# Mixing the work lists of 128 lanes before sorting them again, and issuing the index spread ahead of a group's fetches

## Chip, cores and metric

One core of one Trainium2 chip. The metric is device time in microseconds (us) of one execution; the time before is a median of three runs.

## What is computed

A two-layer network over 64 samples of 256 tokens with 256 features, so 16,384 tokens. Layer 0 is a graph convolution and an LSTM, layer 1 a graph convolution and a feed-forward block. The change touches one piece of that last block, the "tropical" product, which takes a maximum where a matrix product takes a sum:

```python
def blk_fn(xx):                                   # xx: tokens x 256, after a layer norm
    t = jnp.max(xx[:, None, :] + Wt[None, :, :], axis=-1) + bt     # tokens x 1024
    z = t[:, :, None]
    cvx = jnp.max(z * sl_cvx[None] + of_cvx[None], axis=-1)
    ccv = jnp.min(z * sl_ccv[None] + of_ccv[None], axis=-1)
    return s * cvx + (1.0 - s) * ccv
trop = jax.lax.map(blk_fn, xb).reshape(T, FFN)
classical = jax.nn.gelu(xf @ Wc + bc, approximate=False)
g = jax.nn.sigmoid(xf @ Wg + bg)
out = (g * trop + (1.0 - g) * classical) @ Wd + bd
```

The tokens that reach it are normalised rows of a network that starts from normally distributed inputs. The only parts that treat the position of a token in its sample differently are the LSTM and its running sums, which enter with weights near 0.001.

## The kernel before

The tropical product is not computed over all 256 features. For a token, only features whose value plus the largest weight of that feature is high can hold the maximum. `tropical_first` handles the four best features of each half (128 features, `k` = 0 or 1) of all tokens and counts in `done_count[lane, tile, k]` how many of the 128 features of each half are thereby proved irrelevant; a token-half with less than 128 is open, and 128 minus the count is how many features it still needs. Token `128 * tile + lane` sits on lane (partition) `lane`; there are `TILES` = 128 tiles, so each lane has a list of 128 token-halves for each half.

`tropical_plan` (DVE, with two small turns on PE) builds a key from the need and the tile number, counts per lane how many keys need more than 8, 6, 4, 3, 2 and 0 features, takes the maximum over the 128 lanes of each count, and sorts each lane's list in descending order (16 rounds of `max`, which finds eight, and `match_replace`, which strikes them out). Nothing else runs beside it.

`tropical_slots` then runs once for each half. A slot takes the next entry of each lane's sorted list, so one slot works on 128 token-halves. `CLASSES = (16, 8, 6, 4, 3, 2)`: a slot of class g fetches g features for every lane. The number of slots up to the end of each class is the longest lane's count, rounded up to an even number (slots run in pairs) and at least two more than the class before. Each class is a loop of its own on PE, ACT, DVE and POOL.

- DVE: `select` finds the eight (or sixteen) best features of a slot (`ts_top`, `ts_place`) and writes their numbers to `ts_cand` (L2169). `use` (L2180) merges one fetched column of 1024 into the result.
- PE: `spread` (L2103) turns the numbers of a group of up to four features into `ts_index`; it waits for `selected`, that is for the `select` of the slot that it belongs to. `fetch` (L2112) is four matmuls of 512 columns, one-hot times weights, into one of three `ts_fetched` buffers (`RING = 3`); it waits until DVE has used what was in the buffer.
- ACT: `turn_hot` (L2084, L2087) makes `ts_onehot` of the index.
- POOL: for each slot a gather of `t`, a gather of the inputs `y` for three slots on, and a scatter of the result.

The order on DVE is written by hand. Before each slot's uses stands the select of the next:

```python
for j in range(2):
    dve.wait_ge(fetched_used, first + j * g + RING)
    select(i + j + 1, 1 - j, (i + 2 * j) * 8 + 16, 2 if g > CAND else 1)
    for c in range(g):
        use(first, j, g, c, (i + 2) * 8)
```

`tropical_general` treats token-halves that need more than 16 features (here a single placeholder round), and the feed-forward stage follows.

Of the kernel before, what the change touches and what calls it, by code (L numbers as in the profile page):

```python
# [6 lines left out]
F32 = mybir.dt.float32  # L7
BF16 = mybir.dt.bfloat16
F32R = mybir.dt.float32r
ALU = mybir.AluOpType  # L10
ACT = mybir.ActivationFunctionType
AX = mybir.AxisListType
ds = bass.ds

P = 128
B, N, D = 64, 256, 256
KD = D // P
NT = N // P
TOK = B * N
# [1256 lines left out]
CAND = 8  # L1276
TILES = TOK // P
# [8 lines left out]
STEEPEST = 40.0  # L1286
EXP_SPAN = 74.0
ROUND = 12582912.0
FT8 = FFN // P
CH = 512  # L1290
GRP = 4
# [556 lines left out]
def tropical_plan(nc, v):  # L1848


    with ExitStack() as ctx:
        def sb(name, shape, dt=F32):
            return ctx.enter_context(nc.sbuf_tensor("tp_" + name, shape, dt))

        def sem(name):
            return ctx.enter_context(nc.semaphore("tp_" + name))
# [4 lines left out]
        key, left_key, sorted_key = (sb(n, [P, KD, TILES]) for n in ("key", "leftkey", "sortedkey"))  # L1861
        above = sb("above", [P, C, TILES])
        whole, is_open = sb("whole", [P, KD, TILES]), sb("isopen", [P, KD, TILES])
        order, row, from_row, no_token, no_token2 = (
            sb(n, [P, KD, SLOTS]) for n in ("order", "row", "fromrow", "notoken", "notoken2"))
        count, most = sb("count", [P, C]), sb("most", [C, 1])
# [2 lines left out]
        dense = sb("dense", [1, 2])  # L1869
        ps_count = ctx.enter_context(nc.psum_tensor("tp_pscount", [C, P], F32))  # L1870
        ps_most = ctx.enter_context(nc.psum_tensor("tp_psmost", [1, C], F32))
        done_count, rows, ident = (v[n] for n in ("done_count", "rows", "ident"))
        counted, count_turned, most_ready, most_turned = (
            sem(n) for n in ("counted", "count_turned", "most_ready", "most_turned"))
        steps = Steps(sem("steps"), 1)
        block = ctx.enter_context(nc.Block())

        @block.tensor
        def _(pe):
            pe.wait_ge(counted, 1)  # L1880
            pe.transpose(ps_count[:, :], count[:, :], ident[:, :]).then_inc(count_turned, 1)
            pe.wait_ge(most_ready, 1)
            pe.transpose(ps_most[:, :], most[:, :], ident[0:C, 0:C]).then_inc(most_turned, 1)

        @block.vector
        def _(dve):
            def then(instruction):

                dve.wait_ge(steps.sem, steps.done(instruction))

            steps.begin(0)
            then(dve.tensor_scalar(key[:, :, :], done_count[:, :].rearrange("p (s k) -> p k s", k=KD),
                                   -2.0 * P, 2.0 * P * P, ALU.mult, ALU.add))
            for k in range(KD):
                last = dve.tensor_tensor(key[:, k, :], key[:, k, :], v["tile_no"][:, 0:TILES], ALU.add)
            then(last)

            for c, g in enumerate(CLASSES[1:] + (0, CLASSES[0])):
                last = dve.tensor_scalar(above[:, KD * c:KD * c + KD, :], key[:, :, :], 2.0 * P * (g + 1), None, ALU.is_ge)
            then(last)  # L1900
            dve.tensor_reduce(count[:, :], above[:, :, :], AX.X, ALU.add).then_inc(counted, 1)

            src = key
            for r in range(TILES // 8):
                eight = slice(8 * r, 8 * r + 8)
                for k in range(KD):
                    last = dve.max(sorted_key[:, k, eight], src[:, k, :])
                then(last)
                for k in range(KD):
                    last = dve.match_replace(left_key[:, k, :], sorted_key[:, k, eight], src[:, k, :], -1.0)  # L1910
                then(last)
                src = left_key
                if r == 0:
                    dve.wait_ge(count_turned, 1)
                    dve.tensor_reduce(most[:, :], ps_count[:, :], AX.X, ALU.max).then_inc(most_ready, 1)

            then(dve.tensor_scalar(whole[:, :, :], sorted_key[:, :, :], 0.5 / P, -0.25, ALU.mult, ALU.add))
            then(dve.tensor_scalar(whole[:, :, :], whole[:, :, :], ROUND, None, ALU.add))
            then(dve.tensor_scalar(whole[:, :, :], whole[:, :, :], ROUND, None, ALU.subtract))
            dve.tensor_scalar(is_open[:, :, :], sorted_key[:, :, :], 2.0 * P, None, ALU.is_ge)  # L1920
            then(dve.scalar_tensor_tensor(whole[:, :, :], whole[:, :, :], -2.0 * P, sorted_key[:, :, :], ALU.mult, ALU.add))
            then(dve.memset(order[:, :, TILES:SLOTS], 0.0))
            then(dve.tensor_tensor(order[:, :, 0:TILES], whole[:, :, :], is_open[:, :, :], ALU.mult))

            dve.tensor_scalar(row[:, :, :], order[:, :, :], -1.0, float(P), ALU.add, ALU.mult)
            for r in range(2):
                dve.tensor_scalar(no_token2[:, :, :].rearrange("p k (s r) -> p (k s) r", r=2)[:, :, r],
                                  order[:, :, :].rearrange("p k (s r) -> p (k s) r", r=2)[:, :, r],
                                  0.0, float(TOK + (2 + r) * P), ALU.is_equal, ALU.mult)
            then(dve.tensor_scalar(no_token[:, :, :], order[:, :, :], 0.0, float(TOK + P), ALU.is_equal, ALU.mult))  # L1930
            then(dve.tensor_scalar(row[:, :, :], row[:, :, :], v["p_plus"][:, :], None, ALU.add))
            then(dve.tensor_tensor(from_row[:, :, :], row[:, :, :], no_token[:, :, :], ALU.add))
            then(dve.tensor_tensor(row[:, :, :], row[:, :, :], no_token2[:, :, :], ALU.add))
            for k in range(KD):
                dve.tensor_scalar(rows[k][:, :, 0], from_row[:, k, :], float(KD), float(k), ALU.mult, ALU.add)
                dve.tensor_copy(rows[k][:, 1:SLOTS, 1], from_row[:, k, 0:SLOTS - 1])
# [31 lines left out]
def tropical_slots(nc, v, half, left_dram, t_dram):  # L1968


    RING = 3
# [4 lines left out]
    with ExitStack() as ctx:  # L1976
        def sb(name, shape, dt=F32):
            return ctx.enter_context(nc.sbuf_tensor(f"ts{half}_{name}", shape, dt))

        def sem(name):  # L1980
            return ctx.enter_context(nc.semaphore(f"ts{half}_{name}"))
# [114 lines left out]
        @block.tensor  # L2096
        def _(pe):
            def spread(s, j, r, b, n):

                pe.wait_ge(selected, s + 1)  # L2100
                for c in range(n):
                    one = cand[j][:, r * GRP + c:r * GRP + c + 1].to_broadcast([P, P])
                    mm = pe.matmul(index[b][:, c * P:(c + 1) * P], one, ident_b[:, :], start=True, stop=True)  # L2103
                mm.then_inc(index_ready, 1)

            def fetch(first, c, total, b, at):

                buf, ago = ring(c, total)
                pe.wait_ge(fetched_used, first + c + 1 + RING - ago)
                for h in range(FFN // CH):  # L2110
                    for part in range(2):
                        mm = pe.matmul(fetched[buf][:, h * CH:(h + 1) * CH], one_hot[b][:, at * P:(at + 1) * P],  # L2112
                                       w_part[part][:, half, h * CH:(h + 1) * CH],
                                       start=(part == 0), stop=(part == 1))
                mm.then_inc(fetched_ready, 1)

            def slot_pair(i, g, first, hot):
                sizes = groups(g)
                for j in range(2):
                    for r, n in enumerate(sizes):  # L2120
                        q = j * len(sizes) + r
                        b = q % 2
                        pe.wait_ge(one_hot_ready, hot + q + 1)
                        for c in range(n):
                            if c == 2:
                                spread_next(i, j, r, b, sizes)
                            fetch(first, j * g + r * GRP + c, 2 * g, b, c)
                        if n <= 2:
                            spread_next(i, j, r, b, sizes)

            def spread_next(i, j, r, b, sizes):

                if r < len(sizes) - 1:
                    spread(i + j, j, r + 1, 1 - b, sizes[r + 1])
                else:
                    spread(i + j + 1, 1 - j, 0, 1 - b, sizes[0])

            spread(0, 0, 0, 0, GRP)
            classes(pe, slot_pair)

        @block.vector
        def _(dve):
# [39 lines left out]

            def slot_pair(i, g, first, hot):
                for j in range(2):
                    dve.wait_ge(fetched_used, first + j * g + RING)
                    select(i + j + 1, 1 - j, (i + 2 * j) * 8 + 16, 2 if g > CAND else 1)
                    for c in range(g):
                        use(first, j, g, c, (i + 2) * 8)

            select(0, 0, 16, 2)  # L2190
            classes(dve, slot_pair)


# [523 lines left out]
```

## Time and profile before

| | |
|---|---|
| time, median of 3 runs | 6708.94 us (6705.71 to 6711.29) |
| time of the profiled execution | 6724.72 us |
| its span, first to last instruction | 6722.9 us |
| TensorE clock granted, mean | 0.959 |
| PE matmul busy | 5978.2 us (89%) |
| DVE busy | 5148.0 us (77%) |
| ACT busy | 3296.8 us (49%) |
| POOL busy | 1789.5 us (27%) |

Times in the rows are counted from the first instruction. The plan lies from 4144 to 4185 us, the slots of the first half from 4203 to 4775, those of the second from 4801 to 5104. A granted clock of 1 is 2.4 GHz, 0.5 is 1.2 GHz, and what lies between is a mean over time at the two. PE is the matmul side of TensorE, PEld its weight loads.

### The profile page before, as it was taken

The numbers are of one execution on the slowest core, as the hardware profiler recorded it, in microseconds if no ns is written. First come the engines' busy times: TensorE is split into PE (matmuls) and PEld (weight loads), VectorE is DVE, ScalarE is ACT, GpSimd is POOL, SyncE is SP. The second block draws the span as 40 slices with busy tenths as digits, with TensorE's granted clock in tenths as the row PEclk, the third lists the DMA queues.
The fourth block names the chain that finished last, engine by engine and source line by source line (L and its number), as shares of the span: only waits on it lengthen the run. The fifth ranks groups of instructions, "written<-read, shape, count | busy, mean of one in ns | idle before, by whom it ended". The sixth has DMA issues, their size and how long they took to land. (4 is left out here: it accounts for less than half of the span.)

```text
span 6722.9 us, 104063 instructions
## 1 busy us (share of the span) xinstructions
PE 5978.2 (89%) x29554; PEld 4157.6 (62%) x29554; DVE 5148.0 (77%) x9496; ACT 3296.8 (49%) x6081; POOL 1789.5 (27%) x3698
## 2 busy tenths in 40 slices
PE   9998999999988884699999996876675999999999
PEld 6667999999977773466666664544443444444444
DVE  8993333333358888799999998998785999999998
ACT  6662222222234442466666664221122877787777
POOL 3330000000014442465656564247463000000000
PEclk9999999999989997899999998998887999999999
DMA  4440000000024442222121221246354222212221
GB/s 137 134 131 18 0 0 0 0 0 0 0 81 151 154 154 94 82 71 75 70 75 70 75 73 57 67 142 221 136 199 159 67 82 79 79 67 81 77 80 49
DMA packets 366380, 552.30 MB, mean 82 GB/s; under 512 B 29264, under 2 KB 299216, under 8 KB 366288
## 3 DMA queue, kind: packets, MB, share of 16 engines
q1 hardware_dynamic: 322944, 400.58, 18.2%
q0 software_dynamic: 43344, 150.64, 6.6%
q8 instruction: 40, 0.66, 0.0%
q14 instruction: 52, 0.43, 0.0%
HBM read 310.46 MB, written 240.67 MB: 82 GB/s over the span
## 5 line engine op out<-in xcount | busy, mean ns | idle before, releaser
L1710 PE MATMUL t_fetched<-t_wpart,t_onehot 128*128 128x512 f32 x4096 | 1221.6, 420 | 35.7 <-DVE t_tout L1815 15.5
L1815 DVE SCALAR_TENSOR_TENSOR t_tout<-t_fetched,t_top,t_tout 128x1024 f32<-128x1024 f32 x896 | 1149.3, 1283 | 35.5 <-PE t_fetched L1710 4.5
L580 PEld LDWEIGHTS l_ps<-hx,l_whh 128*128 128x128 f32 x8192 | 962.7, 193 | 16.8 <-DVE hx L521 3.7
L580 PE MATMUL l_ps<-hx,l_whh 128*128 (+1 forms) x8192 | 950.7, 275 | 3.2 <-DVE hx L521 3.2
L1710 PEld LDWEIGHTS t_fetched<-t_wpart,t_onehot 128*128 128x128 f32 x4096 | 690.7, 188 | 269.4 <-DVE t_tout L1815 131.0
L2112 PE MATMUL ts_fetched<-t_wpart,ts_onehot 128*128 128x512 f32 x2008 | 632.7, 450 | 209.2 <-ACT ts_onehot L2087 82.4
L545 ACT ACTIVATE l_act<-l_ps 128x128 f32<-128x128 f32 x1024 | 283.6, 277 | 1055.0 <-PE l_ps L580 1055.0
L2606 DVE SCALAR_TENSOR_TENSOR f_line<-f_hinge,f_vec,f_line 128x1024 f32<-128x1024 f32 x512 | 656.8, 1283 | 50.6 <-ACT f_hinge L2490 36.2
L2112 PEld LDWEIGHTS ts_fetched<-t_wpart,ts_onehot 128*128 128x128 f32 x2008 | 380.8, 207 | 397.8 <-DVE ts_tout L2180 232.6
L512 DVE TENSOR_TENSOR l_ig<-l_act 128x128 f32<-128x128 f32 x256 | 74.8, 292 | 592.3 <-ACT l_act L545 592.3
L2540 PE MATMUL f_pso<-f_fused,f_wd 128*128 128x512 f32 x1024 | 469.6, 602 | 36.8 <-DVE f_fused L2593 36.8
L567 PE MATMUL l_ps<-hx,l_wih 128*128 (+1 forms) x2048 | 497.5, 386 | 1.0 <-DVE l_ps L505 1.0
L2180 DVE SCALAR_TENSOR_TENSOR ts_tout<-ts_fetched,ts_top,ts_tout 128x1024 f32<-128x1024 f32 x374 | 480.2, 1284 | 23.3 <-PE ts_fetched L2112 5.6
L2527 PE MATMUL f_psc<-f_x,f_wc 128*128 128x512 f32 x1024 | 483.1, 594 | 0.2 <-ACT f_cls L2475 0.2
L2527 PE MATMUL f_psg<-f_x,f_wg 128*128 128x512 f32 x1024 | 481.2, 592 | 0.0
L2084 ACT ACTIVATE ts_dist<-ts_index,t_pminus 128x512 f32<-128x512 f32 (+2 forms) x168 | 97.3, 579 | 759.2 <-PE ts_index L2103 524.2
L2490 ACT ACTIVATE f_hinge<-f_pst,f_vec 128x1024 f32<-128x1024 f32 x384 | 398.5, 1113 | 0.0
L567 PEld LDWEIGHTS l_ps<-hx,l_wih 128*128 128x128 f32 x2048 | 369.8, 190 | 41.5 <-issue 1.8
L2540 PEld LDWEIGHTS f_pso<-f_fused,f_wd 128*128 128x128 f32 x1024 | 194.4, 192 | 295.6 <-issue 272.6
L775 POOL MEMSET g_half<- 128x2 f32 x1 | 0.1, 99 | 1395.5 <-POOLq L56 1395.5
L2527 PEld LDWEIGHTS f_psg<-f_x,f_wg 128*128 128x128 f32 x1024 | 194.6, 190 | 245.2 <-issue 245.2
L2606 DVE SCALAR_TENSOR_TENSOR f_line<-f_spare,f_vec,f_line 128x1024 f32<-128x1024 f32 x224 | 287.8, 1285 | 44.0 <-DVE f_line L2606 44.0
(379 smaller groups left out, 10666.6 us busy)
## 6 DMA issues: line engine op xcount, KB each, us to landing
t<-t_tout SPq DMA_DIRECT2D x128, 512.0 KB, 2.6
f_t<-t SPq DMA_DIRECT2D x64, 1024.0 KB, 5.2
g_adj<-in_adj SPq DMA_DIRECT2D x128, 256.0 KB, 3.0
g_adjt<-in_adjt SPq DMA_DIRECT2D x128, 256.0 KB, 2.8
t_x<-x_normalised SPq DMA_DIRECT2D x130, 128.0 KB, 2.3
g_x<-in_x SPq DMA_DIRECT2D x64, 256.0 KB, 2.8
x_kept<-g_x SPq DMA_DIRECT2D x64, 256.0 KB, 2.2
g_x<-x_kept SPq DMA_DIRECT2D x64, 256.0 KB, 2.8
```

The lines of the kernel that those rows point to most:

```text
L545: act.activation(act_g[q][:, :, :], ps_g[s][q][:, :, r, :], ACT.Tanh if q == 0 else ACT.Sigmoid)\
L567: pe.matmul(ps_g[s][q][:, c2, :, :], w_ih[:, k, row:row + P], hx[:, k, ds(S * group + 1, S), :], start=False, stop=False, skip_group_check ...
L580: mm = pe.matmul(ps_g[s][q][:, c2, r, :], w_hh[:, k, row:row + P], hx[:, k, ds(t, 1), :].rearrange("p o b -> p (o b)"), start=False, stop= ...
L1710: mm = pe.matmul(fetched[c % RING][:, h * CH:(h + 1) * CH], one_hot[g][:, c % GRP * P:(c % GRP + 1) * P], w_part[part][:, k, h * CH:(h + 1 ...
L1815: dve.scalar_tensor_tensor(t_out[j][:, :], column[:, :], value, t_out[j][:, :], ALU.add, ALU.max)\
L2084: act.activation(dist[b][:, 0:n * P], index[b][:, 0:n * P], ACT.Abs, bias=v["p_minus"][:, :])\
L2112: mm = pe.matmul(fetched[buf][:, h * CH:(h + 1) * CH], one_hot[b][:, at * P:(at + 1) * P], w_part[part][:, half, h * CH:(h + 1) * CH], sta ...
L2180: dve.scalar_tensor_tensor(t_out[j][:, :], column[:, :], top[j][:, c:c + 1], (t_out if c else t_in)[j][:, :], ALU.add, ALU.max).then_inc(f ...
L2490: op = act.activation(hinge[v][:, k, :], ps_t[:, :], ACT.Relu, bias=column(u, "knot", k))
L2527: mm = pe.matmul(ps_[:, :], w_[:, k, u * P:(u + 1) * P], x[j][:, k, h * HB:(h + 1) * HB], start=(k == 0), stop=(k == KD - 1))
L2540: mm = pe.matmul(ps_o[k][:, h * HB:(h + 1) * HB], w_d[:, u, k * P:(k + 1) * P], fused[u % 2][:, h * HB:(h + 1) * HB], start=(u == 0), stop ...
L2606: dve.scalar_tensor_tensor(acc[:, :], source, column(u, "bend", k), acc[:, :], ALU.mult, ALU.add)\
```

## The change

Three things.

1. The plan gives each key the whole token number, sorts each lane's list, then mixes the sorted lists between lanes on PE: the entry of rank t of lane p + 4 (t mod 32) goes to lane p. It counts and takes the maxima on the mixed lists, and sorts them a second time.
2. In the slots DVE's loop body is `use` first and then `select` of the slot two ahead, with two selects ahead of the loops in place of one.
3. On PE the `spread` of the next group stands ahead of the first fetch of a group (`c == 0`). Before, it stood behind the second fetch.

```diff
+            pe.wait_ge(ident2_ready, 1)
+            pe.wait_ge(lanes_sorted, 1)
+            by_turn = [t[:, :, :].rearrange("p k (r m) -> p m k r", m=TURNS) for t in (sorted_key, ps_turned)]
+            for m in range(TURNS):
+                mm = pe.matmul(by_turn[1][:, m, :, :], ident2[:, m * (P // TURNS):m * (P // TURNS) + P],
+                               by_turn[0][:, m, :, :], start=True, stop=True)
+            mm.then_inc(lanes_turned, 1)
...
+            def turnable():
+                for r in range(2):
+                    last = dve.tensor_copy(ident2[:, r * P:(r + 1) * P], ident[:, :])
+                last.then_inc(ident2_ready, 1)
+                for r in range(3):
+                    last = dve.tensor_scalar(spare_row[:, r:r + 1], v["p_plus"][:, :], float(TOK + r * P + 1), None, ALU.add)
+                then(last)
...
+            descending(key, turnable)
+            dve.sem_inc(lanes_sorted, 1)
+
+            dve.wait_ge(lanes_turned, 1)
+            then(dve.tensor_copy(key[:, :, :], ps_turned[:, :, :]))
...
+            descending(key, find_most)
...
-            dve.tensor_scalar(row[:, :, :], order[:, :, :], -1.0, float(P), ALU.add, ALU.mult)
...
-            then(dve.tensor_scalar(row[:, :, :], row[:, :, :], v["p_plus"][:, :], None, ALU.add))
...
                         for c in range(n):
-                            if c == 2:
+                            if c == 0:
                                 spread_next(i, j, r, b, sizes)
                             fetch(first, j * g + r * GRP + c, 2 * g, b, c)
-                        if n <= 2:
-                            spread_next(i, j, r, b, sizes)
...
                 for j in range(2):
-                    dve.wait_ge(fetched_used, first + j * g + RING)
-                    select(i + j + 1, 1 - j, (i + 2 * j) * 8 + 16, 2 if g > CAND else 1)
                     for c in range(g):
                         use(first, j, g, c, (i + 2) * 8)
-
-            select(0, 0, 16, 2)
+                    dve.wait_ge(fetched_used, first + j * g + g + RING)
+                    select(i + j + 2, j, i * 8 + 32, 2 if g > CAND else 1)
+
+            for j in range(2):
+                select(j, j, 16, 2)
             classes(dve, slot_pair)
```

`descending` is the sort of before as a function, called twice. The remaining edits of the plan change constants of the key and the arithmetic of the row numbers.

## Rows read from the trace of the kernel before

**Rows 1.** Windows: busy time of each engine in the plan and the slots.

```profile
core 0: us, PE busy (x) PEld busy (x) DVE busy (x) ACT busy (x) POOL busy (x), PEclk, DMA share, GB/s
...
4144.00:4185.00 41.00, 1.36 (x6) 0.42 (x4) 31.48 (x158) 0.69 (x4) 2.20 (x5) 0.50 0.01 4
...
4203.00:5108.00 905.00, 656.19 (x2511) 407.87 (x2509) 756.98 (x1312) 183.81 (x334) 468.15 (x905) 0.89 0.47 159
```

**Rows 2.** Windows of L2180 by class: 16, 8, 6, 4, 3, 2; second half from 6.

```profile
core 0: us, DVE busy (x), PEclk, DMA share, GB/s
4203.20:4295.30 92.10, 82.17 (x64) 0.94 0.13 43
4295.30:4388.90 93.60, 82.16 (x64) 0.99 0.28 95
4388.90:4461.50 72.60, 61.62 (x48) 0.98 0.36 123
4461.50:4563.70 102.20, 82.16 (x64) 1.00 0.51 175
4563.70:4605.30 41.60, 30.82 (x24) 0.97 0.62 205
4605.30:4774.70 169.40, 92.44 (x72) 0.78 0.68 236
...
4869.60:4906.10 36.50, 30.82 (x24) 0.92 0.37 123
4906.10:4932.00 25.90, 20.55 (x16) 0.96 0.51 172
4932.00:4963.20 31.20, 23.11 (x18) 0.96 0.63 210
4963.20:5103.60 140.40, 77.03 (x60) 0.79 0.68 235
```

**Rows 3.** Timeline of the plan, DVE: first and last step of the sort.

```profile
4153.81 0.48 DVE L1907 MAX8 tp_sortedkey<-tp_key 128x8 f32<-128x128 f32 x2
...
4172.72 0.29 DVE L1917 TENSOR_SCALAR tp_whole<-tp_sortedkey 128x256 f32<-128x256 f32 x1
```

**Rows 4.** Timeline of an earlier stage: 16 weight loads of eight fp32 matmuls.

```profile
2660.54 3.48 PEld L1131 LDWEIGHTS h_pskey<-h_diagonal,h_ones 128*128 128x128 f32 x16 [61.49 <-issue]
```

**Rows 5.** Timeline, class 4: end of a select, spread, first use, next fetch.

```profile
4499.58 0.17 DVE L2169 CAST ts_cand<-ts_place 128x8 bf16<-128x8 uint32 x1
4499.80 0.23 PEld L2103 LDWEIGHTS ts_index<-t_identb,ts_cand 128*128 128x128 bf16 x4 [0.30 <-DVE ts_cand L2169]
4499.81 0.40 PE L2103 MATMUL ts_index<-t_identb,ts_cand 128*128 128x128 bf16 x4
4499.91 1.28 DVE L2180 SCALAR_TENSOR_TENSOR ts_tout<-ts_fetched,ts_top,ts_tin 128x1024 f32<-128x1024 f32 x1 [0.16 <-issue]
4499.99 0.78 PEld L2112 LDWEIGHTS ts_fetched<-t_wpart,ts_onehot 128*128 128x128 f32 x4
...
4501.23 3.92 DVE L2180 SCALAR_TENSOR_TENSOR ts_tout<-ts_fetched,ts_top,ts_tout 128x1024 f32<-128x1024 f32 x3
```

**Rows 6.** Timeline: fetch to the waiting DVE, clock high.

```profile
5137.55 1.20 PE L2267 MATMUL tg_fetched<-t_wpart,tg_runrows 128*128 128x512 f32 x4 [1.19 <-DVE tg_acc L2301]
5138.98 1.28 DVE L2301 SCALAR_TENSOR_TENSOR tg_acc<-tg_fetched,tg_y,tg_acc 128x1024 f32<-128x1024 f32 x1 [0.30 <-PE tg_fetched L2267]
```

**Rows 7.** Timeline, class 2: two fetches to the waiting DVE, clock low.

```profile
4669.64 3.78 PE L2112 MATMUL ts_fetched<-t_wpart,ts_onehot 128*128 128x512 f32 x8 [4.33 <-ACT ts_onehot L2087]
4671.75 1.28 DVE L2180 SCALAR_TENSOR_TENSOR ts_tout<-ts_fetched,ts_top,ts_tin 128x1024 f32<-128x1024 f32 x1 [2.15 <-PE ts_fetched L2112]
...
4673.54 1.28 DVE L2180 SCALAR_TENSOR_TENSOR ts_tout<-ts_fetched,ts_top,ts_tout 128x1024 f32<-128x1024 f32 x1 [0.51 <-PE ts_fetched L2112]
```

**Rows 8.** Timeline, class 2, POOL: the scatters of two slots in a row.

```profile
4656.35 1.00 POOL L2060 DMA_INDIRECT t<-ts_tout,ts_now  x1 [0.16 <-issue]
...
4660.69 1.00 POOL L2060 DMA_INDIRECT t<-ts_tout,ts_now  x1 [0.16 <-issue]
```

More of the change, by code:

```diff
@@ L1288 @@
 ROUND = 12582912.0
+OPEN_ONE = 32768.0
+TURNS = 32
 FT8 = FFN // P
@@ L1863, in tropical_plan @@
         whole, is_open = sb("whole", [P, KD, TILES]), sb("isopen", [P, KD, TILES])
+        ident2, token_no, spare_row = sb("ident2", [P, 2 * P]), sb("tokenno", [P, TILES]), sb("sparerow", [P, 3])
         order, row, from_row, no_token, no_token2 = (
@@ L1871, in tropical_plan @@
         ps_most = ctx.enter_context(nc.psum_tensor("tp_psmost", [1, C], F32))
+        ps_turned = ctx.enter_context(nc.psum_tensor("tp_psturned", [P, KD, TILES], F32))
         done_count, rows, ident = (v[n] for n in ("done_count", "rows", "ident"))
@@ L1874, in tropical_plan @@
             sem(n) for n in ("counted", "count_turned", "most_ready", "most_turned"))
+        ident2_ready, lanes_sorted, lanes_turned = (sem(n) for n in ("ident2_ready", "lanes_sorted", "lanes_turned"))
         steps = Steps(sem("steps"), 1)
@@ L1889, in then, with descending @@
                 dve.wait_ge(steps.sem, steps.done(instruction))
+            def descending(src, between):
+                for r in range(TILES // 8):
+                    eight = slice(8 * r, 8 * r + 8)
+                    for k in range(KD):
+                        last = dve.max(sorted_key[:, k, eight], src[:, k, :])
+                    then(last)
+                    for k in range(KD):
+                        last = dve.match_replace(left_key[:, k, :], sorted_key[:, k, eight], src[:, k, :], -1.0)
+                    then(last)
+                    src = left_key
+                    if r == 0:
+                        between()
@@ new lines, in turnable, with find_most @@
+            def turnable():
[4 more added lines that the diff above has]
+                    last = dve.tensor_scalar(spare_row[:, r:r + 1], v["p_plus"][:, :], float(TOK + r * P + 1), None, ALU.add)
+                then(last)
+            def find_most():
+                dve.wait_ge(count_turned, 1)
+                dve.tensor_reduce(most[:, :], ps_count[:, :], AX.X, ALU.max).then_inc(most_ready, 1)
@@ L1891, in _ @@
             steps.begin(0)
+            dve.tensor_scalar(token_no[:, :], v["tile_no"][:, 0:TILES], float(P), v["p_plus"][:, :], ALU.mult, ALU.add)
             then(dve.tensor_scalar(key[:, :, :], done_count[:, :].rearrange("p (s k) -> p k s", k=KD),
-                                   -2.0 * P, 2.0 * P * P, ALU.mult, ALU.add))
+                                   -OPEN_ONE, OPEN_ONE * P - (P - 1), ALU.mult, ALU.add))
             for k in range(KD):
-                last = dve.tensor_tensor(key[:, k, :], key[:, k, :], v["tile_no"][:, 0:TILES], ALU.add)
+                last = dve.tensor_tensor(key[:, k, :], key[:, k, :], token_no[:, :], ALU.add)
@@ L1896, in _ @@
             then(last)
+            descending(key, turnable)
+            dve.sem_inc(lanes_sorted, 1)
+            dve.wait_ge(lanes_turned, 1)
+            then(dve.tensor_copy(key[:, :, :], ps_turned[:, :, :]))
             for c, g in enumerate(CLASSES[1:] + (0, CLASSES[0])):
-                last = dve.tensor_scalar(above[:, KD * c:KD * c + KD, :], key[:, :, :], 2.0 * P * (g + 1), None, ALU.is_ge)
+                last = dve.tensor_scalar(above[:, KD * c:KD * c + KD, :], key[:, :, :], OPEN_ONE * (g + 1), None, ALU.is_ge)
@@ L1900, in _ @@
             then(last)
             dve.tensor_reduce(count[:, :], above[:, :, :], AX.X, ALU.add).then_inc(counted, 1)
[L1903 to L1915, printed above, removed]
@@ L1917, in _ @@
-            then(dve.tensor_scalar(whole[:, :, :], sorted_key[:, :, :], 0.5 / P, -0.25, ALU.mult, ALU.add))
+            descending(key, find_most)
+            then(dve.tensor_scalar(whole[:, :, :], sorted_key[:, :, :], 1.0 / OPEN_ONE, -0.25, ALU.mult, ALU.add))
             then(dve.tensor_scalar(whole[:, :, :], whole[:, :, :], ROUND, None, ALU.add))
             then(dve.tensor_scalar(whole[:, :, :], whole[:, :, :], ROUND, None, ALU.subtract))
-            dve.tensor_scalar(is_open[:, :, :], sorted_key[:, :, :], 2.0 * P, None, ALU.is_ge)
@@ L1921, in _ @@
-            then(dve.scalar_tensor_tensor(whole[:, :, :], whole[:, :, :], -2.0 * P, sorted_key[:, :, :], ALU.mult, ALU.add))
+            dve.tensor_scalar(is_open[:, :, :], sorted_key[:, :, :], OPEN_ONE, None, ALU.is_ge)
+            then(dve.scalar_tensor_tensor(whole[:, :, :], whole[:, :, :], -OPEN_ONE, sorted_key[:, :, :], ALU.mult, ALU.add))
             then(dve.memset(order[:, :, TILES:SLOTS], 0.0))
             then(dve.tensor_tensor(order[:, :, 0:TILES], whole[:, :, :], is_open[:, :, :], ALU.mult))
-            dve.tensor_scalar(row[:, :, :], order[:, :, :], -1.0, float(P), ALU.add, ALU.mult)
+            dve.tensor_scalar(no_token[:, :, :], order[:, :, :], 0.0, spare_row[:, 0:1], ALU.is_equal, ALU.mult)
@@ L1926, in _ @@
             for r in range(2):
[L1927 to L1930, printed above, removed]
-            then(dve.tensor_scalar(row[:, :, :], row[:, :, :], v["p_plus"][:, :], None, ALU.add))
@@ L1932, in _ @@
-            then(dve.tensor_tensor(from_row[:, :, :], row[:, :, :], no_token[:, :, :], ALU.add))
-            then(dve.tensor_tensor(row[:, :, :], row[:, :, :], no_token2[:, :, :], ALU.add))
+                last = dve.tensor_scalar(no_token2[:, :, :].rearrange("p k (s r) -> p (k s) r", r=2)[:, :, r],
+                                         order[:, :, :].rearrange("p k (s r) -> p (k s) r", r=2)[:, :, r],
+                                         0.0, spare_row[:, 1 + r:2 + r], ALU.is_equal, ALU.mult)
@@ L1934, in _ @@
+            then(last)
+            dve.scalar_tensor_tensor(from_row[:, :, :], order[:, :, :], -1.0, no_token[:, :, :], ALU.add, ALU.add)
+            then(dve.scalar_tensor_tensor(row[:, :, :], order[:, :, :], -1.0, no_token2[:, :, :], ALU.add, ALU.add))
             for k in range(KD):
```

## Prediction

> **What bounds the kernel now.** I read the windows by stage first. The plan takes 41 us in which DVE is busy 31.5 and every other engine less than 2.5 [rows 1]: whatever it grows by is added to the end. The slots take 905 us with DVE busy 757, PE 656, POOL 468 [rows 1], and are the larger sum, so I read them by class. The uses (L2180) in a window, divided by the class, are its slots: 4, 8, 8, 16, 8, 36 in the first half (80), and 4, 4, 6, 30 for classes 6, 4, 3, 2 of the second [rows 2]; its classes 16 and 8 stand at their least size of two each, 48 slots in all. Time per slot is 23.0, 11.7, 9.08, 6.39, 5.20 and 4.71 us; in the second half 9.12, 6.48, 5.20 and 4.68 for the last four. Uses follow each other every 1.32 us [rows 5], so class 4 is 5.28 of uses and 1.1 of select and handover: DVE sets the pace, for PE has the first fetch ready before the select ends. There the use starts 0.16 us after the cast that ends a select (4499.75), before any later fetch is loaded [rows 5]. Class 2 is different: 2.64 of uses and 1.1 give 3.75, yet a slot takes 4.7. POOL's chain of two gathers and a scatter repeats every 4.34 us [rows 8], and for part of the time the clock is low, a mean of 0.78 against 0.97 to 1.00 in classes 3 and 4 of the first half [rows 2].
>
> **The change: shorter lists.** The classes end where the longest of 128 lanes ends: after 4, 12, 20, 36, 44, 80 slots, and 2, 4, 8, 12, 18, 48 [rows 2]. By the reference tokens hardly depend on their position, so I take a lane's count as a draw of 128 with mean m and spread s = sqrt(m(1 - m/128)); the longest of 128 such is about m + 2.6 s. An end at 80 gives m = 65 (s = 5.7, 65 + 14.7). After mixing, neighbouring ranks of a lane's list come from different lanes, so its length is a sum of independent yes or no, "is that lane longer than this rank"; their variances add up to half the mean distance of two draws, 0.56 s. The longest is then m + 2.6 sqrt(0.56 s) = 65 + 4.6, hence 70. The second half: 48 gives m = 34.4, after it 38.8; I take 38. In the same way the ends become 4 or 2, 8, 14, 28, 36, 70 and 2, 4, 6, 8, 12, 38. With 4 as the first end, 4 slots of class 8, 2 of class 6, 2 of class 4 and 2 of class 2 go in the first half: 4 x 11.7 + 2 x 9.08 + 2 x 6.39 + 2 x 4.71 = 87. In the second 2, 2, 2 and 4 of classes 6, 4, 3, 2: 18.2 + 13.0 + 10.4 + 18.7 = 60. If the first end is 2, two slots turn from class 16 into 8, 22.6 more; at even odds 11. Together **-159 us**. The longest lane itself scatters by 2 or 3, so -125 to -190.
>
> **The plan.** The sort takes 18.9 us [rows 3]; a second is +18.6 (the step between its rounds is moved, not doubled). The 32 fp32 matmuls: no row has their shape. The nearest are eight fp32 statements that show 16 loads in 3.48 us at the low clock, 0.217 a load, two a statement [rows 4]. 64 loads are 13.9 us at the low clock, at which PE stands through the plan [rows 1], or 7 if it rises; I take 13.9. Copying the identity, spare rows, token numbers, the copy back and two handovers between engines I put at 1.9 by DVE steps of 0.3 us like that in [rows 3], and two removed steps of this size at -0.7. Together **+33 us** (26 to 36), nothing beside it.
>
> **DVE's order.** Written out, the order before is S0, S1 U0, S2 U1, S3 U2 (S select, U uses); after, S0 S1, U0 S2, U1 S3. These are the same. "Two ahead" only counts from another place: S(s+1) still runs between U(s-1) and U(s), behind the same uses, for the same `y`, which POOL gathers at the same point. Only S1 moves ahead of the loops' start. Price 0 to +1 for each half; I take 1 in all.
>
> **PE's order.** Here a wait is added to the path. With classes 4, 3 and 2 a slot is one group, and its `spread_next` belongs to slot s+1 and waits for S(s+1), which ends just before U(s). Before, one or two fetches of slot s stood ahead of that wait. Now all of them are queued behind it: fetch 0 of slot s can't begin until S(s+1) has ended, and DVE, which has nothing else to do, waits for it. The handover from cast to first use was 0.1 (mean of 0.16 and 0). At the high clock it becomes 0.05 to the spread, 0.19 until the fetch's load [rows 5] and 1.43 from fetch to DVE [rows 6], 1.67. A slot becomes 1.0 + 1.67 + 4 x 1.32 = 7.95 (class 4), 6.58 (3), 5.21 (2; POOL's 4.34 no longer binds): +1.56, +1.38, +0.52. At the low clock DVE starts 2.11 after the fetch and the next column follows after 1.79 [rows 7]: with a spread twice as long, 2.54 + 3 x 1.79 + 1.32 + 1.0 = 10.23, and 8.35 and 6.46: +3.84, +3.15, +1.77. After the shorter lists 16, 12 and 60 slots are left: +73 us if always high, +205 if always low. Between them I go by class 2 of before, the row with the most idle PE, where the clock was low for 0.44 of the time (mean 0.78) [rows 2]. A stop of PE now stands in every slot of three classes, so half of the slots low in classes 4 and 3, two thirds in class 2: 16 x 2.70 + 12 x 2.27 + 60 x 1.35 = **+151 us**. In classes 6, 8 and 16 the wait is for a select that ended before the slot's uses: 0. What the earlier spread gives back, PE's wait for ACT's one-hot in class 2, is in these sums, which have none.
>
> The Trainium skill, "TensorE: Matmul & The Clock Gate", section "Part 2: What happens when you issue a matmul", lets a weight load be pulled ahead of matmuls in flight. If the fetch's load passed the spread, 0.19 us of each of 88 slots, 17 us, would be saved. The rows show loads behind a spread in program order and do not show one passing it, so the sum leaves it out.
>
> Sum: -159 + 33 + 1 + 151 = **+26 us**. The profiled execution took 6724.7 us with a span of 6722.9, 16 above the median; on the median of 6709 it gives **6735 us**.
>
> **Rivals.**
> A, faster: PE's clock stays high in the single-group classes. For: it was 0.97 to 1.00 in classes 4 and 3. Against: 0.78 in class 2, with less of a stop than now. -159 + 34 + 73 = -52, so 6657. It decides from 1.4 us a slot: a stop below that (125 / 88) makes the kernel faster.
> B, the clock falls and stays low there: -159 + 34 + 205 = +80, 6789. Against: no class was low throughout. The Trainium skill, "TensorE: Matmul & The Clock Gate", section "A second HAM failure mode: psum-queue depth-cycling", has frequent short idles swing the clock between its levels; by that rule the sum lies between A and B, and the trace agrees with 0.78 in class 2.
> C, lanes differ by more than chance (by position in the sample). The means would lie lower and more slots go, say ten more of class 2 in each half: 20 x 4.7 = 94 more saved and 27 less of stop, -253 + 34 + 124 = -95, 6614. Against: the reference.
> D, the lists do not shorten, because the lengths were already equal: nothing saved, and the stop in 20, 14 and 66 slots, +34 + 175, 6918. Against: 128 random lists are not equal; I keep the weaker form, half the shortening: -80 + 34 + 163 = +117, 6826.
>
> **Numbers.** Chances: forecast 0.52, A 0.16, B 0.12, C 0.12, D 0.08. The forecast's own range is 6695 to 6775, from the lists' 33 either way and 110 to 190 for the stop. The range that should hold 8 in 10 is 6665 to 6800: it takes in B and most of the way to A, and leaves out C, D and a part of A. About 0.2% (13 us) is what a measurement of this kernel can tell from no change. Slower by more: B, D and 0.37 of the forecast's 0.52, 0.57. Within it: 0.10 of the forecast and a part of A's upper edge, 0.13. Faster: 0.30.
>
> **What the profile will show.** Right: a plan near 75 us with 64 fp32 loads; ends near 70 and 38 (about 108 slots, 410 uses instead of 502); in class 4 each slot's first L2180 waiting about 1.5 us for `ts_fetched`, with no L2112 between the last use and the L2103 of the next slot; a clock below 0.9 in classes 4 and 3; unchanged times a slot in classes 6, 8 and 16. Wrong: first uses that still start 0.1 us after the cast, a clock of 0.97 in class 4, or ends far from 70 and 38.

## Result and the profile after

The changed kernel takes **6756.5 us** (median of 4 runs, 6749.9 to 6759.4); the kernel before took 6709.6 beside it (4 runs). The ratio is 1.007, with a 95% interval of 1.0057 to 1.0083: slower by 0.7%, or 47 us, where 6735 (26 us more) was forecast. The profiled execution took 6759.4, with a span of 6756.6; its clock was 0.94 over the span.

Windows of the changed kernel by engine, its plan from the end of the first sort and its slots:

```profile
core 0: us, PE busy (x) PEld busy (x) DVE busy (x) ACT busy (x) POOL busy (x), PEclk, DMA share, GB/s
4172.00:4238.20 66.20, 16.64 (x75) 15.40 (x76) 33.63 (x179) 2.63 (x4) 6.46 (x9) 0.50 0.07 19
4238.20:5131.00 892.80, 590.81 (x2005) 390.69 (x2004) 612.89 (x1106) 148.27 (x276) 388.53 (x750) 0.76 0.39 133
```

Beside [rows 1] the stage of the slots, with the stretch between its halves, is only 12 us shorter, though DVE has 144 us less to do in them and PE 65 less: both have become idler, and the mean clock has fallen from 0.89 to 0.76. By class, windows of the uses (L2206, which was L2180); the second half begins at 4848.90:

```profile
core 0: us, DVE busy (x), PEclk, DMA share, GB/s
4238.20:4333.50 95.30, 82.16 (x64) 0.93 0.13 44
4333.50:4357.10 23.60, 20.55 (x17) 1.00 0.26 87
4357.10:4450.00 92.90, 77.02 (x60) 1.00 0.36 121
4450.00:4519.90 69.90, 41.08 (x32) 0.79 0.38 130
4519.90:4595.00 75.10, 38.51 (x30) 0.73 0.43 147
4595.00:4815.60 220.60, 92.44 (x72) 0.61 0.52 179
4848.90:4895.10 46.20, 41.08 (x32) 0.96 0.12 38
4895.10:4918.70 23.60, 20.54 (x16) 1.00 0.28 96
4918.70:4938.00 19.30, 15.40 (x12) 1.00 0.34 116
4938.00:4956.90 18.90, 10.27 (x8) 0.68 0.38 132
4956.90:4987.30 30.40, 15.40 (x12) 0.72 0.42 144
4987.30:5131.00 143.70, 61.62 (x48) 0.64 0.52 182
```

Uses divided by the class give the slots: 4, 2, 10, 8, 10, 36 (70) and 2, 2, 2, 2, 4, 24 (36), against 80 and 48 [rows 2]. The first list ends where the forecast put it, at 70, the second at 36 where 38 was forecast. From the first use of one slot to that of the next, averaged by class, it is 23.8, 11.8, 9.36, 8.77, 7.50 and 6.17 us in the first half. The wide classes changed little (by 0.1 to 0.8 us), and a slot of classes 4, 3 and 2 has become 2.4, 2.3 and 1.5 us longer than in [rows 2].

The reason stands in the timeline, class 4 with the clock at its high level (2.4 GHz); to be read beside [rows 5]:

```profile
4503.61 1.28 DVE L2206 SCALAR_TENSOR_TENSOR ts_tout<-ts_fetched,ts_top,ts_tin 128x1024 f32<-128x1024 f32 x1 [1.58 <-PE ts_fetched L2140]
...
4509.74 0.17 DVE L2195 CAST ts_cand<-ts_place 128x8 bf16<-128x8 uint32 x1
4509.97 0.23 PEld L2131 LDWEIGHTS ts_index<-t_identb,ts_cand 128*128 128x128 bf16 x4 [4.11 <-DVE ts_cand L2195]
...
4510.18 3.26 PE L2140 MATMUL ts_fetched<-t_wpart,ts_onehot 128*128 128x512 f32 x9
...
4511.56 1.28 DVE L2206 SCALAR_TENSOR_TENSOR ts_tout<-ts_fetched,ts_top,ts_tin 128x1024 f32<-128x1024 f32 x1 [1.64 <-PE ts_fetched L2140]
```

The first and last row are the first uses of two slots in a row. PE's loads stand idle for 4.11 us until the cast that ends the select. PE then spreads, and only after that does it fetch. DVE waits 1.64 us for the first column, where it waited 0.16 us before, put down to "issue" (nothing that the profile shows). At the low level (1.2 GHz), class 2:

```profile
4809.31 0.40 PE L2131 MATMUL ts_index<-t_identb,ts_cand 128*128 128x128 bf16 x2 [2.53 <-DVE ts_cand L2195]
...
4811.73 1.28 DVE L2206 SCALAR_TENSOR_TENSOR ts_tout<-ts_fetched,ts_top,ts_tin 128x1024 f32<-128x1024 f32 x1 [2.47 <-PE ts_fetched L2140]
...
4813.36 1.28 DVE L2206 SCALAR_TENSOR_TENSOR ts_tout<-ts_fetched,ts_top,ts_tout 128x1024 f32<-128x1024 f32 x1 [0.34 <-PE ts_fetched L2140]
```

The first use comes 2.47 late and the second another 0.34. The plan's new part is one block, in the timeline of PE:

```profile
4170.73 13.79 PE L1889 MATMUL tp_psturned<-tp_sortedkey,tp_ident 128*128 128x8 f32 x64 [25.21 <-DVEq L1936]
```

It is 32 fp32 products in 64 passes of 0.215 us at the low clock; 13.9 was forecast from [rows 4]. From the start of the plan to the end of the last sort it is 57.2 us (DVE: 4150.20 to 4207.41), where it was 23.2.

### The profile page after: what moved, and what is told of

It reads as the page before. It is cut to its first block and busy times, and to the rows that moved or that the text cites. A ratio compares the mean times of both kernels' runs of the same rounds, so it can differ in the third digit from the quotient of the medians.

```text
span 6756.6 us, 102279 instructions
## 1 busy us (share of the span) xinstructions
PE 5928.7 (88%) x29118; PEld 4156.9 (62%) x29118; DVE 5023.2 (74%) x9391; ACT 3265.2 (48%) x6025; POOL 1712.4 (25%) x3544
## 5 line engine op out<-in xcount | busy, mean ns | idle before, releaser
L2140 PE MATMUL ts_fetched<-t_wpart,ts_onehot 128*128 128x512 f32 x1608 | 571.8, 506 | 48.1 <-DVE ts_tout L2206 36.8
L2112 ACT ACTIVATE ts_dist<-ts_index,t_pminus 128x256 f32<-128x256 f32 (+2 forms) x140 | 79.5, 568 | 817.2 <-PE ts_index L2131 670.7
L2206 DVE SCALAR_TENSOR_TENSOR ts_tout<-ts_fetched,ts_top,ts_tout 128x1024 f32<-128x1024 f32 x296 | 380.0, 1284 | 38.8 <-PE ts_fetched L2140 30.5
```

The lines of the kernel that those rows point to most:

```text
L2112: act.activation(dist[b][:, 0:n * P], index[b][:, 0:n * P], ACT.Abs, bias=v["p_minus"][:, :])\
L2206: dve.scalar_tensor_tensor(t_out[j][:, :], column[:, :], top[j][:, c:c + 1], (t_out if c else t_in)[j][:, :], ALU.add, ALU.max).then_inc(f ...
```

## The experiments

The experiments were run in four batches (x1 to x4, x5 to x7, x8 to x10, x11 and x12), in which the kernel before took 6706.9, 6712.1, 6723.0 and 6722.1 us. So times are compared as ratios to the runs of before in the same batch; 0.001 is 6.7 us. The three columns on the right are from one trace of each kernel. "Plan" is from DVE's first step of it to its last, "slots" the sum of both halves, from the first use to the end of the last, and "last stage" the time from the first write of `f_pst` to the end.

| kernel | us | ratio [95%] | plan | slots | last stage |
|---|---|---|---|---|---|
| before | 6709.6 | 1 | 34.3 | 871.4 | 1562.2 |
| after | 6756.5 | 1.0070 [1.0057, 1.0083] | 67.7 | 856.7 | 1562.2 |
| x1_mix_only | 6599.9 | 0.9840 [0.9824, 0.9856] | 67.7 | 690.8 | 1571.8 |
| x2_slots_only | 6909.6 | 1.0302 [1.0285, 1.0319] | 34.3 | 1045.6 | 1572.9 |
| x3_mix_select | 6600.3 | 0.9840 [0.9824, 0.9857] | 67.7 | 698.6 | 1563.0 |
| x4_mix_spread | 6762.3 | 1.0084 [1.0067, 1.0101] | 67.7 | 852.6 | 1571.6 |
| x5_sort_twice_unmixed | 6757.7 | 1.0069 [1.0053, 1.0086] | 67.7 | 857.0 | 1573.8 |
| x6_fill_clock | 6696.9 | 0.9975 [0.9963, 0.9986] | 67.7 | 795.8 | 1563.2 |
| x7_mix_turns8 | 6610.6 | 0.9850 [0.9834, 0.9867] | 57.5 | 714.7 | 1572.1 |
| x8_spread_second | 6620.7 | 0.9846 [0.9830, 0.9863] | 67.7 | 719.3 | 1562.2 |
| x9_mix_turns16 | 6622.7 | 0.9852 [0.9835, 0.9868] | 60.8 | 722.0 | 1562.3 |
| x10_mix_longer_dve | 6609.5 | 0.9832 [0.9816, 0.9849] | 68.9 | 703.4 | 1564.6 |
| x11_select_again | 6614.3 | 0.9841 [0.9827, 0.9854] | 67.7 | 711.3 | 1562.8 |
| x12_longer_again | 6611.4 | 0.9839 [0.9826, 0.9852] | 68.9 | 705.9 | 1563.4 |

**Theory**: the lists gain what was forecast, and the spread ahead of fetch 0 takes it back, by holding fetch 0 and by the clock that falls with PE's stops. **Rivals**: the new plan or the longer reach of the select costs it; or the lists gain little.

**The change in its parts.** x1 is the changed plan with the slots of before, x2 the plan of before with the changed slots. x3 adds DVE's new order to x1, x4 adds PE's:

```diff
 x3: slot_pair and start of the vector block as in the change
-                    dve.wait_ge(fetched_used, first + j * g + RING)
-                    select(i + j + 1, 1 - j, ...)      # before the uses
+                    dve.wait_ge(fetched_used, first + j * g + g + RING)
+                    select(i + j + 2, j, ...)          # behind the uses
 x4: fetch loop of the tensor block as in the change
-                            if c == 2:
+                            if c == 0:
...
-                        if n <= 2:
-                            spread_next(i, j, r, b, sizes)
```

x1: 

> The changed plan (mixed lists, two sorts) with the slots as they were before. Theory T (lists save, the plan costs, the whole loss is in the new order of the slots): ends of 70 and 36 slots, saving 162 us at the class prices of before, plan +34, so about 6710 - 128 = 6582 us. Rival M (rows scattered over tokens make gathers and scatters slower): class 2 takes clearly more than the 4.7 us a slot of before, and the time is well above 6600.

x2: 

> The plan as before, with the changed slots (use first and select two ahead; spread ahead of the first fetch). Theory T: the lists of before (80 and 48 slots) with 8.74, 7.5 and 6.1 us a slot in classes 4, 3 and 2 as the changed kernel shows: 20 x 2.35 + 14 x 2.3 + 66 x 1.4 = 171 us more, 7 for the loop's turn in the wider classes and 12 for the two exits, about 6900 us. Rival: the stop belongs to the mixed lists and not to the order; then about 6710.

x3: 

> The changed plan and the changed order on DVE (use first, select two ahead), with the spread where it was before. Theory T: DVE runs the same sequence, so only the loop's turn between a select and a use (0.5 us a pair) and the exit of each half (6 us) are paid: 6582 + 18 = 6600 us. Rival D (DVE's order makes the stop): near the changed kernel's 6757.

x4: 

> The changed plan and the spread ahead of the first fetch, with DVE's order as before. Theory T: the whole stop, 6757 less 18 = 6740 us, with first uses waiting 1.6 to 2.5 us for a fetch in classes 4, 3 and 2. Rival D (DVE's order makes the stop): 6582, first uses 0.1 us behind the cast.

Without the early spread the changed plan is 1.6% faster than before (x1, x3); with it 0.8% slower (x4) or 0.7% (the changed kernel), so hardly by DVE's order. With the longer lists of before (x2, 20, 14 and 66 slots in these classes) it costs the more: 189 us of slots above the 857.0 of x5 (below), which has these lists and the slots of before. From x3 to the changed kernel the ratio rises by 0.0230, 154 us, and the slots by 158. Windows of the uses of x3, classes 4, 3 and 2 of the first half (columns as above):

```profile
4447.80:4499.90 52.10, 41.08 (x32) 0.97 0.50 171
4499.90:4551.80 51.90, 38.50 (x30) 1.00 0.60 209
4551.80:4711.40 159.60, 92.43 (x72) 0.83 0.72 247
```

With the same uses, 70, 75 and 221 us have become 52, 52 and 160, and the clock is back at 0.97, 1.00 and 0.83. x1, x2 and x4 came out 18, 10 and 22 us above what was expected of them, and x3 did not; that is taken up below.

**The plan without its gain.** x5 sorts twice and sends every lane back to itself. It leaves the mixing out.

```diff
 x1, and
-                mm = pe.matmul(by_turn[1][:, m, :, :], ident2[:, m * (P // TURNS):m * (P // TURNS) + P],
+                mm = pe.matmul(by_turn[1][:, m, :, :], ident2[:, 0:P],
```

> The changed plan with every one of the 32 matmuls taking the same identity, so no entry leaves its lane; slots as before. It leaves the mixing out and keeps its work. Theory T: ends of 80 and 48 as before, and only the plan's price: 6710 + 34 = 6744 us. Rival (sorting twice or the new keys alone shorten the lists): fewer slots and less time.

The lists end at 80 and 48 again, so sorting twice shortens nothing by itself. The plan costs 33.4 us; of the 45.6 us above before (34 were expected), 11.6 are the last stage's. From x5 to x1, which differ in the turn alone, the slots fall by 166 us: this is what mixing gives. Nor do the rows, now scattered over tokens, slow the gathers and scatters: a slot of class 2 takes 4.43 us in x1 and 4.44 in x5.

**The clock's share.** x6 is the changed kernel with products that nobody reads behind the fetches of each one-group slot, written to the bank of the slot's own spread, which is done with by then:

```diff
+            def fill(b, n):
+                for _ in range(n):
+                    for part in range(4):
+                        pe.matmul(index[b][:, 0:CH], one_hot[b][:, 0:P],
+                                  w_part[part % 2][:, half, 0:CH], start=True, stop=True)
...
+                        if g <= GRP:
+                            fill(b, 1 if g == 2 else 2)
```

> The changed kernel with 4 (class 2) or 8 (classes 3 and 4) more matmuls of 512 columns behind each slot's fetches, where PE stands idle; their results are never read. Theory T (a good half of the stop is the clock that falls because PE stands): the granted clock in classes 4, 3, 2 rises from 0.79, 0.73, 0.61 to above 0.9, a slot takes about 7.95, 6.6 and 5.3 us, and the time falls by 16 to 10 x 0.8 + 14 x 0.9 + 60 x 0.8, some 65 us, to about 6690. Rival (the clock is not what the idle time sets, or the wait is PE's queue alone): the time stays at 6757 or rises by the work added.

Windows of the uses, the same three classes:

```profile
4451.90:4516.80 64.90, 41.08 (x32) 0.93 0.39 131
4516.80:4581.70 64.90, 38.51 (x30) 1.00 0.50 170
4581.70:4775.80 194.10, 92.44 (x72) 0.87 0.59 204
```

PE does more, and the kernel is 0.95% faster than the changed one (0.9975 against 1.0070, 64 us). That is what the clock gives back of the 154, and the clock is then near x3's (0.93, 1.00 and 0.87, against 0.97, 1.00 and 0.83); the other 91 are the handover itself. The added products don't hold the next fetch back: in 56 of the 84 slots of these classes the first use starts 1.51 to 1.60 us after the cast, and the shortest such time in the changed kernel is 1.52. In class 3, at 1.00, the wait is still there, in the timeline of x6:

```profile
4536.51 1.28 DVE L2215 SCALAR_TENSOR_TENSOR ts_tout<-ts_fetched,ts_top,ts_tin 128x1024 f32<-128x1024 f32 x1 [1.59 <-PE ts_fetched L2140]
```

**One fetch ahead.** x8 is the changed kernel with the spread one fetch later where a slot is one group:

```diff
-                            if c == 0:
+                            if c == (1 if n == g else 0):
```

> The changed kernel with one statement moved: in the one-group classes (4, 3 and 2) PE queues the next slot's spread ahead of fetch 1 instead of ahead of fetch 0. If the 156 us between the changed kernel and the one with the spread at its old place are the stop of fetch 0 behind the next select, nearly all of it goes: fetch 0 runs during the select, and only fetch 1 comes late, by 1.67 us less the 1.32 of the first use, 0.35 us a slot at the high clock in 16, 14 and 60 slots, 30 us: 6630 (6610 to 6680, the upper end where the clock stays low in class 2). If the cost comes from anything else that the early spread does (its product written beside fetches, ACT's one-hot made earlier, DVE's order), it stays near 6757, or at least above 6700.

Timeline of x8, class 4:

```profile
4457.19 1.28 DVE L2206 SCALAR_TENSOR_TENSOR ts_tout<-ts_fetched,ts_top,ts_tin 128x1024 f32<-128x1024 f32 x1
4457.24 0.23 PEld L2131 LDWEIGHTS ts_index<-t_identb,ts_cand 128*128 128x128 bf16 x4 [2.59 <-DVE ts_cand L2195]
...
4458.75 3.92 DVE L2206 SCALAR_TENSOR_TENSOR ts_tout<-ts_fetched,ts_top,ts_tout 128x1024 f32<-128x1024 f32 x3 [0.28 <-PE ts_fetched L2140]
```

The first use follows the cast at once, for fetch 0 was done during the select, and fetch 1 comes 0.28 late. In the first half a slot of class 4 takes 6.87 us against 6.52 in x11 (0.35 was expected), one of class 3 5.55 against 5.20, one of class 2 4.59 against 4.62. Class 2 pays nothing, so of the 30 us that were expected to remain only 3 (ratios) to 8 (slots) do. One statement's place gives back 150 of the 154 us (0.9846 against 1.0070). What else the early spread brings, the one-hot made earlier included, is still there in x8 and costs at most these 3 to 8 us.

**How far the lanes must be mixed.** x7 is x1 with `TURNS = 8`, x9 is x3 with `TURNS = 16`.

x7: 

> The changed plan with TURNS = 8 in place of 32: eight matmuls of 32 columns, rank t comes from the lane 16 x (t mod 8) on; slots as before. Theory T: the dozen ranks round the end of a list still come from different lanes, so the ends stay at 70 and 36 to 38, and the plan loses 48 of 64 weight loads of 0.215 us: 10.3 us less than the kernel with the changed plan alone, about 6572. Rival: mixing over eight lanes is too coarse, and the lists grow by more slots than the 10 us pay.

x9: 

> Changed plan and changed DVE order with the spread at its old place, and the lanes turned in 16 steps instead of 32: 16 products of 128 x 8 x 2 fewer, 32 loads of 0.215 us, so the plan is 6.9 us shorter. Against TURNS = 8, which ended 4 and 2 slots later than 32, 16 turns mix 16 lanes of every 8th: if the ends come out as with 32, 6593; if a pair of class 2 comes back in one half, about 6602.

x7's plan is 10.2 us shorter as expected, but the lists end at 74 and 36, two slots of class 2 in the second half have turned into class 3, and the slots take 24 us more. (The expectation of x9 counts two more slots in the second half of x7; the trace has 36.) In x9 the turn takes 6.98 instead of 13.79 us:

```profile
4171.92 6.98 PE L1889 MATMUL tp_psturned<-tp_sortedkey,tp_ident 128*128 128x16 f32 x32 [25.21 <-DVEq L1936]
```

and the lists end at 72 and 36. That is two more slots, and two of class 6 turned into 8 and two of class 2 into 3: the slots take 10.7 us longer than in x11. The ratio is 0.9852, where 6602 us or 0.9840 was the higher of the two values expected. Fewer turns lose more in the lists than they save in the plan, by the traces; the ratios of x9 and x11 have intervals that overlap.

**The stage that should not change.** The last stage (from the first `f_pst` to the end) is the same code in all kernels, yet takes 1562 to 1565 us in nine and 1572 to 1574 in five (x1, x2, x4, x5, x7). Idle time of DVE before the uses of `f_line` in x1, by what ended it (us, times):

```profile
L2634 DVE SCALAR_TENSOR_TENSOR f_line<-f_hinge,f_vec,f_line x512: 1275/1284/1287, 5043.9 to 6582.4; 128x1024 f32<-128x1024 f32 x171
...
  ACT f_hinge L2518: 31.0, 28
  issue: 15.1, 5
```

Five stops of 3 us, put down to no other engine. The five kernels are those in which one of DVE's two parts, plan and slots, is new and the other old, and it is not the same part in all (x2). So the length of DVE's program, and with it where the last stage lies in it, is a suspect. x10 lengthens x1's program by 20 short copies, 1.2 us of plan:

```diff
 x1, with sparerow 23 columns wide, and in turnable():
+                for r in range(20):
+                    dve.tensor_copy(spare_row[:, 3 + r:4 + r], v["p_plus"][:, :])
```

> Changed plan with the slots of before, as in the first experiment (6599.9), and 20 copies of 128 x 1 on DVE in the plan whose result nobody reads, which make DVE's program 20 instructions longer. If the 10 us by which the last stage was longer there (five stops of DVE of some 3 us, 195 us apart, that are put down to issue) come from where that stage's instructions lie in DVE's program, they go and the stage takes 1562 us again: 6591. If they come from what the slots left behind, it stays 1572, and with the 1.3 us of the copies 6601.

The same groups of x10:

```profile
L2636 DVE SCALAR_TENSOR_TENSOR f_line<-f_hinge,f_vec,f_line x512: 1276/1285/1287, 5056.7 to 6587.9; 128x1024 f32<-128x1024 f32 x171
...
  ACT f_hinge L2520: 37.4, 36
```

The stops are gone and the stage takes 1564.6. The traces also show what happens in the stops. The page of the profile has a queue for instructions, q14, with its packets, MB and share. It carries more in the kernels with stops; x1, then x10:

```profile
q14 instruction: 78, 0.64, 0.0%
q14 instruction: 53, 0.43, 0.0%
```

Between 400 and 1300 us of the last stage it brings 22 pieces of 8 KB in each of the five kernels with stops and none in the nine without. In all 25 stops a piece starts to arrive 1.0 to 1.3 us after DVE has stopped (x1: DVE stands from 5422.55 to 5425.51, a piece arrives at 5423.58). So in five kernels instructions are loaded at every turn of this stage's loop, about 194 us long, and DVE stands while one piece comes; in the others the loop runs without loading. The trace does not say whose instructions a piece holds, but of x1 and x10 only DVE's program differs. Why 20 instructions ahead of the loop decide it is not shown.

This is where x1, x2, x4, x5 and x7 lost some 10 us of what was expected, and why x1 and x3 came out equal though their slots differ by 7.8 us. The last two runs put that to the test:

x11: 

> The kernel of the third experiment (changed plan, DVE's new order, spread at its old place) once more, beside the next one on one chip, to price DVE's order where the last stage takes the same time in both. If putting the select ahead of the loop's turn costs what the traces of the first and third experiments show, 690.8 against 698.6 us of slots, it takes 4 us more than the next one (7.8 less the 1.3 us of copies and the 2.4 us that the last stage kept there): 0.9839 against 0.9833 of before. If DVE's order is free, it takes 4 us less than the next one.

x12: 

> The kernel of the tenth experiment (changed plan, slots of before, 20 more instructions in DVE's program) once more, beside the one before. Slots of 691 us in all if DVE's order makes the difference, 698 if it does not; its time 4 us below the other's, or 4 above it.

The slots are 5.4 us longer in x11 and the time 3.0, with intervals that overlap: by the medians alone the sign is not settled. The traces of both pairs agree, though. In class 4 most pairs of slots take 12.77 us from first use to first use in x1 and x12, and 13.00 to 13.06 in x3 and x11. DVE's order costs 5 to 8 us. In x1 DVE's first use of every other slot of classes 16 to 3 starts 0.16 us after the cast, in x3 after 0.5 to 0.7. In x3 the select is the last thing in the loop's body, and the turn of the loop stands bare between it and the use. In x1 the turn comes behind a use of 1.28 us, which can cover it. That this is the reason is read from the program, and no run tests it alone.

## Why the prediction was right in sign and where its sum was off

| step | forecast | measured |
|---|---|---|
| shorter lists | -159 | -162 at the prices of [rows 2] with the real ends; -166 from x5 to x1 |
| plan | +33 | +33.4 |
| DVE's order | +1 | +5 to +8 |
| PE's order | +151 | +154 (ratios), +158 (slots) |
| handovers | 0 | +13 |
| sum | +26 | +46; by the medians +47 |

The last column takes -162, 33, 8, 154 and 13. By the traces alone the account closes too: from x5, with the lists and slots of before, to the changed kernel the slots change by -166, +8 and +158, together nothing, and the plan and the handovers make +47.

The prediction has the direction and the main mechanisms right. Its sum is 20 us too low, nearly all of it for two of its steps: the handovers between stages were left out, and DVE's two orders were taken to be the same.

**The lists** were right, with an end at 70 as forecast and 36 for 38, and rivals C and D are refuted. The inner ends of the first half were 6, 16, 24 and 34, where 8, 14, 28 and 36 were forecast; those of the second were as forecast. That -159 and -162 lie so close is partly luck. The forecast has 11 us for even odds of a first end of 2, which came out at 4, and the other ends saved 15 more than it had for them.

**The plan** was right in its sum and its largest term (13.8 for 13.9).

**PE's order** was right as a mechanism, and as a size partly by luck. With 10, 14 and 60 slots left in classes 4, 3 and 2 (16, 12 and 60 were forecast), the changed kernel has 2.4, 2.3 and 1.6 us a slot more than x3; 2.70, 2.27 and 1.35 were forecast. For the real slots the forecast's prices give 140 us, not 151. The prices of classes 3 and 2 also hold slips: by the forecast's own terms a slot takes 6.63 and 5.31 us at the high clock and 8.44 and 6.65 at the low one, not 6.58, 5.21, 8.35 and 6.46. With these the real slots give 150. The price at the high clock was exact: 7.95 us for a slot of class 4, and from 4503.61 to 4511.56 in the timeline above it is 7.95. The share of the low clock was guessed: a mean of 0.75, 0.75 and 0.67 for classes 4, 3 and 2, where the rows show 0.79 and 0.68, 0.73 and 0.72, 0.61 and 0.64. Rival A (the clock stays high, 6657) is shown by x6 to be what the kernel would be worth with PE kept busy, in part: -17 us against before, not -52. The -52 lacks some 20 us of handovers and DVE's order, and even in x6 the clock was 0.87 in class 2. The Trainium skill, "TensorE: Matmul & The Clock Gate", section "A second HAM failure mode: psum-queue depth-cycling", has frequent short idles between groups of matmuls swing the clock and cost throughput; the rows agree (0.83 in class 2 of x3, 0.61 in the changed kernel), and x6 gives the price, 64 us.

**DVE's order** was a step whose reasoning failed: "These are the same." It costs 5 to 8 us where 1 was forecast. The sequence is the same, but not where the loop turns in it. I compared the order of the statements and not what each of the two positions hides.

**The handovers** were not in the sum, and are its largest missing term. The stretch between the halves grew from 27.2 to 34.3 us and the one behind the second from 58.9 to 65.2. Before a block of the program ends, each engine's sequencer executes a DRAIN, and the next block starts behind the last of them, POOL's. By source line, before (L1976) and in the changed kernel (L2004), in ns:

```profile
L1976 POOLq DRAIN  x2: 2427/2915/3403, 4779.3 to 5108.1; - x2
L2004 POOLq DRAIN  x2: 8797/9122/9447, 4820.2 to 5134.8; - x2
```

The first half's grew from 2.43 to 8.80 us and the second's from 3.40 to 9.45, 12.4 of the 13 us. It does not hang on DVE's or PE's order, nor on the plan, but on the number of slots ahead of it. The DRAIN behind a first half of 80 slots takes 2.43 us (before, x2, x5), of 74 slots 0.96 (x7), of 72 slots 9.29 (x9), and of 70 slots 8.80 in all nine kernels with 70. Behind a second half of 48 slots it is 3.40, behind one of 36 slots 9.45 in all eleven. Why its length depends so on the number is open.

Of the profiled execution's own 33.7 us between spans, 13 are missing against the medians. That of before lay 15 us above its median, and its slots took 871.4 us against 857.0 in x5, which has the same slots and lists. The difference is in class 2, 4.73 and 4.69 us a slot against 4.44 in x5. This fits, but there is no second profile of before. Class 2 has two paces in the other runs as well: 4.33 to 4.48 us where before took 6707 to 6712 (x1, x3, x5, x7), and 4.47 to 4.65 where it took 6722 to 6723 (x8 to x12), x3 and x11 being the same kernel. What sets the pace is not shown.

The best of these kernels are x1, x3, x10, x11 and x12 (ratios 0.983 to 0.984, not told apart): the new plan, with fetches ahead of the spread.

## What to carry to other kernels

An instruction put ahead in an engine's queue brought its wait with it. What mattered was not how early its result was wanted but what stood behind it until its operand was there. Here one fetch less behind the spread was worth 2.2% of the kernel. Where an engine's own stops let its clock fall, price the stop at both levels; the second price came to two thirds of the first here. And test a change part by part: a gain of 1.6% and a loss of 2.3% came in as one change of 0.7%, and two equal medians (x1, x3) hid an 8 us loss behind a 9 us one elsewhere.

## What was unexpected

A stage of 1562 us with unchanged code took 7 to 10 us more or less as DVE's program ahead of it was 20 instructions shorter or longer (x1 against x10): five stops of about 3 us, in each of which a piece of 8 KB arrives on the instruction queue.

The handover between two stages took 6 to 7 us more when the stage before it had fewer slots (70 or 72 for 80, 36 for 48), nearly all of it in POOL's DRAIN at the end of a block. With 74 slots it stayed near its length with 80 (28.7 against 28.0 us).
